# Spectral convolution on 8 images: pairs of image rows on one partition, so that a store's runs are 1 KB and not 512 B

## The reference, cut to what matters

```python
x = _L0_conv_ref(x, ...)              # 3x3 filters made of the channel means
x_ht = dht_2d(x)
out_ht = zeros.at[:, :, :M1, :M2].set(compl_mul2d(x_ht[:, :, :M1, :M2], w1))
y = dht_2d(out_ht) / (H * W)
y = gaussian_smoothing_4d(y)
mask = (jnp.abs(jnp.fft.fftfreq(W)) <= CUTOFF)
return y * mask                       # 33 + 33 columns of 128 are not zero
```

## Time and profile before

| | us |
|---|---|
| median of 3 runs | 223.38 |
| lowest and highest | 223.07, 229.33 |
| span of the profiled execution | 224.2 |
| TensorE busy in it | 184.7 |
| VectorE, ScalarE, GpSimd busy | 143.2, 106.0, 78.5 |

### The profile page before, as it was taken

The page is one execution under the profiler, slowest core; times in us unless marked ns, Lnnn a source line. Parts: engine busy times, 40 slices in busy tenths (PEclk is TensorE's granted clock), DMA queues, the critical chain, the costliest instruction groups (busy, mean ns, idle before and its releaser), DMA issues.

```text
span 224.2 us, 3769 instructions
## 1 busy us (share of the span) xinstructions
PE 184.7 (82%) x1274; PEld 109.8 (49%) x1274; DVE 143.2 (64%) x300; ACT 106.0 (47%) x237; POOL 78.5 (35%) x45
## 2 busy tenths in 40 slices
PE   5789995698798999999997999777898988887400
PEld 3136563355354266546564768576555555554200
DVE  0004129999999994862799879908679788753200
ACT  2377750454255233323554210717888888862200
POOL 9970029555767757837476005000000000000000
PEclk9999999589679655556999685999799999999855
DMA  7999999947507506230000000000079999999998
GB/s 192 294 261 311 315 334 337 315 121 196 180 0 194 181 0 187 85 102 0 0 0 1 1 0 0 1 6 0 3 215 280 283 285 282 286 282 281 286 285 234
DMA packets 43792, 37.08 MB, mean 165 GB/s; under 512 B 692, under 2 KB 35676, under 8 KB 43524
## 3 DMA queue, kind: packets, MB, share of 16 engines
q1 hardware_dynamic: 43780, 36.93, 57.3%
HBM read 20.15 MB, written 16.78 MB: 165 GB/s over the span
## 4 chain that ended last, share of the span: by engine, by line
PE 28%; DVE 27%; SPq 12%; ACT 12%; DMA 9%; issue 6%; ACTq 0%; DVEq 0%
ACT modes L572 7%; PE ps L383 6%; SPq L316 5%; PE ps L529 5%; DVE w_acc L829 5%; PE ps L415 5%; DMA w_raw<-mix_w 5%; DVE xht L810 5%; DMA out<-rows 5%; PE ps L393 3%; DVE terms L806 3%; DVE kb_tmp L768 3%; SPq L347 3%; DVE lf_bn L766 3%; PE ps L403 2%
## 5 line engine op out<-in xcount | busy, mean ns | idle before, releaser
L964 POOL TENSOR_TENSOR w_pair<-w_raw 128x640 f32 (+1 forms) x24 | 39.1, 1655 | 28.7 <-DMA w_raw<-mix_w 16.8
L383 PE MATMUL ps<-x_ring,k_wide 128*64 128x512 f32 x128 | 43.3, 762 | 3.3 <-DMA x_ring<-x 3.3
L529 PE MATMUL ps<-cols,k_wide 128*128 128x396 f32 (+2 forms) x96 | 35.3, 505 | 8.8 <-ACT modes L572 4.0
L616 ACT COPY y_sb<-ps 128x448 f32<-128x448 f32 x32 | 29.6, 932 | 21.3 <-PE ps L393 21.3
L611 ACT COPY freq<-ps 128x512 f32<-128x512 f32 x32 | 18.9, 592 | 36.3 <-PE ps L383 36.1
L415 PEld LDWEIGHTS ps<-k_wide,y_sb 128*128 128x128 f32 x192 | 27.9, 224 | 9.4 <-ACT y_sb L616 5.0
L393 PEld LDWEIGHTS ps<-k_wide,freq 128*128 128x128 f32 x128 | 15.9, 160 | 31.4 <-issue 30.2
L572 ACT COPY modes<-x_ring 32x128 f32<-32x128 f32 (+3 forms) x96 | 30.4, 430 | 1.6 <-DVE x_ring L881 0.9
L415 PE MATMUL ps<-k_wide,y_sb 128*128 128x44 f32 x192 | 28.7, 309 | 0.2
L529 PEld LDWEIGHTS ps<-cols,k_wide 128*128 128x128 f32 x96 | 17.2, 196 | 22.0 <-ACT modes L572 8.0
L393 PE MATMUL ps<-k_wide,freq 128*128 128x128 f32 x128 | 25.0, 326 | 0.1
(11 more groups left out here) (68 smaller groups left out, 181.4 us busy)
## 6 DMA issues: line engine op xcount, KB each, us to landing
out<-rows SPq DMA_DIRECT2D x7, 1152.0 KB, 9.4
out<-rows SPq DMA_DIRECT2D x8, 896.0 KB, 8.9
w_raw<-mix_w SPq DMA_DIRECT2D x2, 1200.0 KB, 10.6
out<-rows SPq DMA_DIRECT2D x3, 384.0 KB, 3.2
x_ring<-x SPq DMA_DIRECT2D x2, 512.0 KB, 5.1
k_wide<-wide SPq DMA_DIRECT2D x1, 437.0 KB, 8.5
x_ring<-x SPq DMA_DIRECT2D x15, 0.5 KB, 8.3
k_wide<-wide SPq DMA_DIRECT2D x1, 225.0 KB, 2.7
```

The costliest lines, as they stand in the source:

```text
L383: last = nc.tensor.matmul(ps[half * 64:half * 64 + 64, g % 2, :], const(O_LT, (1, 64)), x_ring[:, u, at:at + G1 // 2 * H], start=True, sto ...
L529: nc.tensor.matmul(ps[:, B_F[k % 3], 0:nt * NW], const(O_LH + s * H, (1, H)), cols[:, u, t:t + nt, :], start=True, stop=True).then_inc(f_d ...
L616: nc.scalar.copy(view(y_sb[:, u, 0, g * G1:g * G1 + 1], (1, G1 // 2), (G1 // 2, 2), (C, NP)), view(ps[:, 2 + g % 2, 0:1], (128, G1 // 2), ...
L964: tt(w_pair[:, k - 1, :, :], lo, hi, ALU.add).then_inc(pairs_done, 1)
```

## The change

The row stage makes the even and the odd image rows apart. Chunk k now is channel s = k // 2 of the triples and row parity r = k % 2. It is made by two matmuls of 64 outputs each: one for triples 0 to 5 into the lower 64 partitions, one for triples 6 to 11 into the upper 64, both with 396 columns. Triple 11 doesn't exist; its place in `cols` is cleared by GpSimd. Partition p of the lower half then holds image rows 2p and 2p+1 of channels 0 to 17, side by side, partition 64 + p those of channels 18 to 31. The constant matrix of the row stage is reordered to fit (even rows, then odd).

A store takes 64 partitions and moves runs of 1 KB: one for the channels of the lower half (1,152 KB), one for those of the upper half (896 KB), issued one behind the other when all six chunks are placed. Image 0 goes in three steps of two such transfers, each after two chunks. The first three chunks now need the column copies of both ScalarE and VectorE.

```diff
-        CHUNKS = [(s, t, (6 if t == 0 else (5 if s < 2 else 4))) for t in (0, 6) for s in range(3)]
-        FIRST = 18
-        PLACED = (1, 3, 3, 4, 5, 5)
-        ROUND = 5
+        PLACED = (1, 1, 2, 2, 3, 3)
+        ROUND = 3
...
-            def store(n, u, lo, hi, placed):
-                sp.wait_ge(rows_act, n * ROUND + placed)
-                sp.wait_ge(rows_dve, n * ROUND + placed)
-                dst = out[bass.ds(n, 1), lo:hi, :, :]
-                sp.dma_start(dst.rearrange("a c h w -> h (a c) w"), rows[:, u, lo:hi, :]
-                             ).then_inc(out_done[u], 16)
+            by_pair = out.rearrange("n c (p r) w -> n p c (r w)", r=2)
+
+            def store(n, u):
+                sp.wait_ge(rows_act, n * ROUND + ROUND)
+                sp.wait_ge(rows_dve, n * ROUND + ROUND)
+                for half in range(2):
+                    lo, hi = (0, 3 * SIDE) if half == 0 else (3 * SIDE, C)
+                    dst = by_pair[bass.ds(n, 1), :, lo:hi, :].rearrange("a p c f -> p (a c) f")
+                    sp.dma_start(dst, view(rows[half * HP:half * HP + HP, u, 0, 0, 0:1], (2 * H, hi - lo), (1, 2 * H))
+                                 ).then_inc(out_done[u], 16)
...
             for s in range(3):
-                sp.wait_ge(rows_dve if s == 1 else rows_act, PLACED[s])
-                sp.dma_start(out[0, s:FIRST:3, :, :].rearrange("c h w -> h c w"), rows[:, 0, s:FIRST:3, :]
-                             ).then_inc(out_done[0] if s == 2 else out_first, 16)
-            store(0, 0, FIRST, C, ROUND)
-            store(1, 1, 0, FIRST, PLACED[1])
-            store(1, 1, FIRST, C, ROUND)
+                sp.wait_ge(rows_act, PLACED[2 * s])
+                sp.wait_ge(rows_dve, PLACED[2 * s + 1])
+                for half in range(2):
+                    lo, hi = (0, 3 * SIDE) if half == 0 else (3 * SIDE, C)
+                    count = len(range(lo + s, hi, 3))
+                    sp.dma_start(by_pair[0, :, lo + s:hi:3, :],
+                                 view(rows[half * HP:half * HP + HP, 0, s, 0, 0:1], (3 * 2 * H, count), (1, 2 * H))
+                                 ).then_inc(out_done[0] if s == 2 else out_first, 16)
+            store(1, 1)
...
                 if part == 0:
                     pe.wait_ge(cols_act, n + 1)
-                else:
                     pe.wait_ge(cols_dve, n + 1)
...
-                    nc.tensor.matmul(ps[:, B_F[k % 3], 0:nt * NW],
-                                     const(O_LH + s * H, (1, H)), cols[:, u, t:t + nt, :],
-                                     start=True, stop=True).then_inc(f_done, 1)
+                    for half in range(2):
+                        last = nc.tensor.matmul(ps[half * HP:half * HP + HP, B_F[k % 3], 0:SIDE * NW],
+                                                const(O_LH + (s * 2 + r) * HP, (1, HP)),
+                                                cols[:, u, half * SIDE:half * SIDE + SIDE, :],
+                                                start=True, stop=True)
+                    last.then_inc(f_done, 1)
...
+            nc.gpsimd.memset(cols[:, :, TRIPLES:, :], 0.0)
-            nc.gpsimd.memset(rows[:, :, :, :], 0.0).then_inc(zeroed, 1)
+            nc.gpsimd.memset(rows[:, :, :, :, :], 0.0).then_inc(zeroed, 1)
```

More of the change, by code:

```diff
@@ L44 @@
 TRIPLES = 11
+SIDE = 6
+HP = H // 2
 BPAD = 32
@@ L184, in constants @@
     wide[:, O_TW:O_LH] = tw
-    wide[:, O_LH:] = lh.transpose(1, 0, 2).reshape(128, -1)
+    wide[:, O_LH:] = lh.transpose(1, 0, 2).reshape(128, 3, HP, 2).transpose(0, 1, 3, 2).reshape(128, -1)
     t, own = np.arange(KROWS) // J, np.kron(np.arange(KROWS) % J, 1)[:, None] == (np.arange(128) // C)[None]
@@ L258, in hartley_conv_kernel @@
         modes = sb("modes", [128, 2, (C + 1) * NF + 1])
-        cols = sb("cols", [128, 2, TRIPLES, NW])
-        rows = sb("rows", [H, 2, C, H])
+        cols = sb("cols", [128, 2, 2 * SIDE, NW])
+        rows = sb("rows", [128, 2, 3 * SIDE, 2, H])
         ps = ctx.enter_context(nc.psum_tensor("ps", [128, 8, 512], fp32))
@@ L358, in _ @@
+            store(1, 1)
             with sp.Fori(1, N // 2) as it:
                 for u in range(2):
-                    store(it * 2 + u, u, 0, FIRST, PLACED[1])
-                    store(it * 2 + u, u, FIRST, C, ROUND)
-            sp.wait_ge(out_first, 32)
+                    store(it * 2 + u, u)
+            sp.wait_ge(out_first, 64)
             for u in range(2):
@@ L517, in to_rows @@
                     pe.wait_ge(cols_act, n + 1)
-                else:
                     pe.wait_ge(cols_dve, n + 1)
                 for k in range(3 * part, 3 * part + 3):
-                    s, t, nt = CHUNKS[k]
+                    s, r = k // 2, k % 2
                     if k >= 3:
@@ L576, in place_rows @@
         def place_rows(copy, k, u):
-            s, t, nt = CHUNKS[k]
-            return copy(view(rows[:, u, 3 * t + s, 0:1], (3 * H, nt), (H - HALF, 2), (1, HALF)),
-                        view(ps[:, B_F[k % 3], 0:1], (NW, nt), (HALF, 2), (1, HALF)))
+            return copy(view(rows[:, u, k // 2, k % 2, 0:1], (3 * 2 * H, SIDE), (H - HALF, 2), (1, HALF)),
+                        view(ps[:, B_F[k % 3], 0:1], (NW, SIDE), (HALF, 2), (1, HALF)))
         def unmix(copy, bank):
@@ L690, in rows_step @@
                     act.wait_ge(f_done, n * 6 + k + 1)
-                    place_rows(nc.scalar.copy, k, u).then_inc(
-                        rows_act, PLACED[k] - (PLACED[k - 2] if k >= 2 else 0))
+                    place_rows(nc.scalar.copy, k, u).then_inc(rows_act, 1)
             def write_step(n, u, it):
@@ L710, in _ @@
             act.wait_ge(turned, 3)
-            act.wait_ge(out_first, 32)
+            act.wait_ge(out_first, 64)
             with act.Fori(1, N // 2 - 1) as it:
@@ L900, in rows_step @@
                     dve.wait_ge(f_done, n * 6 + k + 1)
-                    place_rows(nc.vector.tensor_copy, k, u).then_inc(
-                        rows_dve, PLACED[k] - (PLACED[k - 2] if k >= 2 else 0))
+                    place_rows(nc.vector.tensor_copy, k, u).then_inc(rows_dve, 1)
             def write_step(n, u, it):
@@ L923, in _ @@
             dve.wait_ge(turned, 3)
-            dve.wait_ge(out_first, 32)
+            dve.wait_ge(out_first, 64)
             with dve.Fori(1, N // 2 - 1) as it:
```

## The result

| | before | changed |
|---|---|---|
| median, us (4 runs each) | 223.62 | 239.72 |
| lowest and highest | 223.07, 229.33 | 234.5, 281.75 |
| span of the profiled execution, and its time | 224.2 | 232.7, 234.5 |

The comparison gives 1.057 times the time before, 95% interval 1.046 to 1.069: slower, by 13 us where 20 were forecast. The quiet means here are 236.2 us and, before, 223.4. Compared again, beside the experiments, the ratio was 1.047 (1.035 to 1.059).

A forecast was written before the change was run, and what follows sets the result against it. The store rate was taken to bound: image 1's data from 174.8 us, plus seven images at 9.73 us (68.1) to 242.9, plus 1.0 to the end, less 0.8, gives 243.1 us; range 222 to 250, its own 236 to 250.

The forecast's parts named there:

- The cause: Stretch of stores at the end: the store rate bounds, and a store from half the partitions passes 215.5 GB/s; chance 0.80.
- the waits: Sign in the row copies: ScalarE's and VectorE's waits for stores grow from 13 us together to 30 or more.
- the last copy: Sign at the end of the span: the last copy of rows ends over 10 us before the end.
- 215 GB/s from 175 us on: Sign in the stretch of stores: windows from 175 us give about 215 GB/s with a DMA share near 1.0.
- The rate of the stretch: Stores of the last seven images: 9.73 us each at 215.5 GB/s, 68.1 us in all.
- the middle case: Stretch of stores: a partial limit or an unchanged rate, 222 to 235 us; chance 0.12, of which 0.10 within 2%.
- The start: Beginning of the stores: first data near 163.9 us, data of image 1 at 174.8 us.
- From span to median: End of the sum: profiled span 224.2 us against a median of 223.38, so 0.8 us comes off.
- TensorE: Row matmuls: the two of a pair run side by side, 0.44 us more per image, hidden under the stores.
- Run length: Stores: 1 KB runs give 349 GB/s if nothing else limits, 48.0 us for all stores.
- The first rival: Reading side of stores: the halves' rule doesn't bind, rate 349 GB/s, production binds, near 217 us; chance 0.08.
- The second: Rival on stores: run length buys nothing, halves cost nothing; 284 GB/s stays, 227 us; within the 0.12 for 222 to 235.

The follow-up runs named there:

- turning the order: Changed kernel with the order of its two half stores turned in every other image, so lower follows lower; median 242.80 us.
- the middle partitions: Changed kernel with every store reading partitions 32 to 95, so the upper channels hold what belongs to others; median 223.19 us.
- the run from 128 partitions: Kernel before with neighbouring channels stored as 1 KB runs from all 128 partitions, output places permuted; median 216.13 us, ratio 0.960.
- GpSimd's queue: Changed kernel with the upper half's stores issued by GpSimd; median 238.40 us, ratio 1.073.
- The halves at 512 B: Kernel before with each store split into partitions 0 to 63 and 64 to 127 (image 0's first three steps whole); 224.39 us, ratio 1.007.
- changed again: Changed kernel run again as it is, beside the other experiments on the same chip; median 234.08 us, ratio 1.047.
- a second queue: Changed kernel with the upper half's stores issued by ScalarE (from image 1 on) or by GpSimd; ratios 1.052 and 1.073.

## Why the prediction was right, and where its numbers were off

*The cause* held. The rate of the stores bounds; a store from one half of the partitions passes about 212 GB/s. Shown by the windows after an empty stretch (211, 213, 214), by turning the order (221) and by the middle partitions (347). That the limit is half of 431 GB/s was a guess from a load with other rows. It fits, and a half passed the same with runs of 512 B (214) as with 1 KB (211), but no run shows that 431 is what all partitions can pass. Of the signs that I had named, the waits (34 us for 30 or more) and the last copy (12.6 us before the end for over 10) came; 215 GB/s from 175 us on did not, it was 253 and 237.

*The rate of the stretch* is the term that was mis-sized. I put 215.5 GB/s for all stores, 68.1 us for seven images. Measured, data of image 1 begins near 172.1 (share 0.86 in window 172:173) and ends near 231.2: 59.1 us, 248 GB/s. A half alone costs what I said; but I took the halves as strictly one after the other, and they run partly beside each other. I had that as a question, and the sum answered it with no overlap at all, which no row here carried. So the state that came is in part the middle case, a partial limit, to which I had given 0.12.

*The start.* First data to data of image 1: 10.9 us forecast, 11.3 measured. In place, 172.1 against 174.8, since in this execution everything before the stores was 3.6 us earlier: the first row matmul at 155.86 us in place of 159.42, in a part that the change doesn't touch. That is chance.

*From span to median.* I took 0.8 us off. The changed kernel's profiled execution had 234.5 us with a span of 232.7, so 1.8 us lie around a span (1.7 to 1.9 in every run of the experiments). The execution profiled before was then near 226.0, some 2.6 us above its median, and I mistook that for a constant. The four parts, 2.7 too late, 9.0 too long, 0.5 and 2.6 too short at the end (1.5 us from the last data to the end for 1.0, and this), make the 8.6 us between 243.1 and 234.5. The median of 239.72 is nearer to 243.1 than the mechanism earned, and that is luck: the quiet mean lies 6.9 us below the forecast, at the edge of its own range of 236 to 250, and the one of the second comparison, 231.8, outside it.

*TensorE* as forecast: pairs side by side, 0.89 us; 0.52 us more per image for 0.44 and 0.06 of a copy. *Run length*: 349 GB/s worked out, 337 and 347 measured where no half stands alone. *The first rival* was right on what fast stores would bring (217 forecast, though its own terms add up to 216.3; 216.13 measured, with the shorter production of the kernel before) and wrong in that stores from a half are not fast. *The second*, that the run length buys nothing, is excluded by the run from 128 partitions.

## What to carry to other kernels

The time of a transfer follows which partitions it touches before it follows how long its runs are: 1 KB from the lower or upper 64 partitions in long stores is slower (212 to 253 GB/s) than 512 B from all 128 (284). If a store must take 64 partitions, 32 to 95 read as fast as all of them (347 and 337 GB/s). Where halves can't be avoided, stores of about 512 KB of the two halves in turn, issued before the queue runs dry, bring the rate back to 288, until the issuing (some 0.8 us each) binds.

## What the runs showed that I had not expected

After a dry spell the rate of half stores of 448 KB or more begins at 210 to 214 GB/s (seen seven times, in four kernels; 198 with GpSimd's queue) and climbs: in the changed kernel it takes about 14 us to pass 280, with pieces of about 512 KB about 6. The halves at 512 B, in stores of up to 576 KB, do the same from 214 to 291 GB/s. It fits that the DMA engines drift apart until some read one half while others read the other.

No view of the profile tells the engines apart, but the trace keeps 16 completion signals for each store, as many as there are DMA engines. Taken in order of time, the first and the last of a store's 16 are this far apart:

| stores | us from the first signal to the last |
|---|---|
| before, images 1 to 7 | 0.4 to 0.9, mostly 0.5 |
| changed, image 1 (after the gap) | 0.5 and 1.0 |
| changed, images 2 and 3 | 1.3, 2.2, 2.2 and 3.1 |
| changed, images 4 to 7 | 2.0 to 4.1 |
| changed again, image 6 | 3.7 and 3.9 |
| changed again, image 7 (after the dry spell) | 0.5 and 1.1 |
| all from 32 to 95, images 1 to 7 | 0.4 to 1.3, mostly 0.5 |

With the halves at 512 B the signals come from image 3 on in two groups of eight, about 1.0 to 1.6 us apart. So the engines do drift apart where stores go from one half to the other, and not where every store spans both, and a dry spell brings them together again. That it is this drift which lifts the rate fits in time, and fits the groups of eight; but which half an engine reads isn't recorded, so this last step is argued, not shown. Open is also why a second queue brought so little.
